# Gathering 20 of 731 row sets with TensorE: one-hot matrices times a table split into three bf16 parts

## The chip, the cores and the metric

The kernel runs on one core of a Trainium2 chip. Its time is the device time of one execution in microseconds (us), the median of several. Of the core's engines PE is TensorE, DVE VectorE, ACT ScalarE, POOL GpSimd and SP SyncE; SP computes nothing here and only issues transfers.

## What is computed

A graph of 6250 nodes and 100000 edges sorted by `dst`; D is 256. For each edge a vector from the source's and the destination's rows, then the maximum over the edges of each node, then a residual and a layer norm.

```python
x_src = x[src]
x_dst = x[dst]
theta_x = (x_dst - x_src) @ theta_w.T + theta_b
phi_x = x_src @ phi_w.T + phi_b
e = relu(theta_x + phi_x)
out = segment_max(e, dst, num_segments=x.shape[0])
out = where(isfinite(out), out, 0.0)
return layernorm(x + out)
```

Since `relu` is monotone and the part of `dst` is the same for all edges of a node, the kernel takes the maximum over `B[src]` alone, with B = x (phi - theta), and adds A = x theta + the two biases afterwards.

## The kernel before

The edges are cut into 128 runs of 782 edges, one run to a partition. Step k handles edge k of every run: it needs 128 rows of B (128x256 f32, 128 KB), which an indirect DMA of POOL gathers, and DVE folds them into a running maximum that restarts where `dst` changes (`reset`). The steps go in 261 groups of three.

Before the loop PE makes B in 49 tiles of 128 nodes (L411), ACT copies them out of PSUM (L357), SP writes them to `b_table` in HBM. Meanwhile POOL gathers 51 row sets of x itself into `early` (L303); in groups 0 to 102 PE transposes and multiplies them (L437, L427) and ACT copies them (L368, L366), so that the first step of the groups 6, 8, ... 106 needs no gather from the table. That leaves 731 gathers (L315) into `rows`, which has 18 places: POOL waits with a gather until the step that used its place is folded (`s_fold`).

In a group g of the loop, in the order of each queue: DVE folds three steps (L582), two into PSUM (`acc`) and the third into `hist`; every step waits for the one before through `s_fold`. ACT copies the two from `acc` to `hist` (L379). SP writes the group's three maxima to `runmax` in HBM (L274). The first step of group g waits for the gather and for ACT's copy of group g - 2 (`s_copied`), and a place of `hist` is free again when the write of group g - 6 has landed. Every fourth group up to 196 has a mark as well: two small DVE operations (L596, L601), five PE matmuls with the bf16 halves `hi` and `lo` of `dst` (L447 to L449), one ACT pass over 782 columns (L384). In groups 204 to 252 PE makes one tile of A each (L462) from `xt_sb` tiles that SP loads, and DVE adds the biases into `a_sb` (L631). After the last group the maxima that cross a run are mended, and in a tail of 14 pieces the maximum of each node is gathered from `runmax`, added, normalised and written; none of that is touched.

All queues are written out by hand and run in program order. PE, for one, does in group g: product and transposes of a conversion, the mark, the tile of A.

## Time and profile before

| | us |
|---|---|
| median of 3 runs (lowest, highest) | 1245.99 (1243.34, 1250.09) |
| the profiled execution | 1242.66 |
| its span, first to last instruction | 1240.8 |
| first and last row gather start | 103.8, 1143.6 |

The profile's page gives each engine's busy time, its share in 40 slices, the DMA queues, the chain that ended last and the groups of instructions. A row of the timeline is: start, duration, engine, line, operation, output and inputs, shape, count, and in brackets how long the engine was idle before and what ended that. "remote" and "issue" there mean that the profile shows no releaser.

### The profile page before, as it was taken

How to read it: one execution, taken by the hardware profiler on the slowest of the kernel's cores; microseconds unless marked ns; L12 is line 12 of the kernel's file. 1: busy time of each engine (PE TensorE's matmuls, PEld its weight loads, DVE VectorE, ACT ScalarE, POOL GpSimd, SP SyncE). 2: the span in 40 equal slices, each digit the busy share in tenths (PEclk: the TensorE clock that was granted, in tenths of full speed). 3: DMA queues.
4: the chain of work that ended last, by engine and by line, in shares of the span. 5: the costliest groups of instructions: out<-in, count | busy, mean ns of one | idle time of the engine just before them, and what ended most of it. 6: DMA issues, size and time to landing. Idle time of an engine off the chain costs nothing.

```text
span 1240.8 us, 5980 instructions
## 1 busy us (share of the span) xinstructions
PE 313.0 (25%) x953; PEld 194.2 (16%) x953; DVE 518.0 (42%) x1191; ACT 274.6 (22%) x568; POOL 807.9 (65%) x840
## 2 busy tenths in 40 slices
PE   6363322444342343110000000100014342430000
PEld 5142111222121232000000000000012131210000
DVE  4002332545343454543333433543325253537698
ACT  2022132233232232321111211321101010100144
POOL 6724756766666766677765676677746667667574
PEclk9667565666566655555555555555557565656555
DMA  8567545666465665676655665776547476747264
GB/s 262 164 196 225 178 156 169 229 204 210 159 204 181 215 213 194 231 241 201 199 191 166 209 192 191 256 228 206 192 139 261 145 236 225 240 136 229 100 195 157
DMA packets 111584, 245.76 MB, mean 198 GB/s; under 512 B 19141, under 2 KB 51226, under 8 KB 111546
## 3 DMA queue, kind: packets, MB, share of 16 engines
q0 software_dynamic: 39984, 109.21, 30.8%
q1 hardware_dynamic: 71130, 135.51, 29.9%
q10 hardware_dynamic: 432, 0.66, 0.2%
q14 instruction: 30, 0.25, 0.1%
q8 instruction: 8, 0.13, 0.0%
HBM read 129.89 MB, written 115.45 MB: 198 GB/s over the span
## 4 chain that ended last, share of the span: by engine, by line
DVE 29%; another core or an unknown queue 27%; issue 19%; POOL 10%; PE 6%; ACT 5%; DMA 4%; DVEq 1%; SPq 0%; ACTq 0%; POOLq 0%
DVE acc L582 16%; POOL rows L315 9%; DVE hist L582 6%; ACT hist L379 3%; DMA rows<-b_table,idx 2%; DVE stats L692 1%; PE acc L411 1%; DVE a_sb L681 1%; DVE hist L689 1%; DVE reached L596 1%; DVE a_sb L676 1%; PE ps_b L427 1%; PE ps_a L411 1%; DVEq L580 1%
## 5 line engine op out<-in xcount | busy, mean ns | idle before, releaser
L315 POOL DMA_INDIRECT rows<-b_table,idx x731 | 701.3, 959 | 372.2 <-issue 208.4
L379 ACT COPY hist<-acc 128x512 f32<-128x512 f32 x253 | 147.3, 587 | 471.0 <-DVE hist L582 241.3
L582 DVE SCALAR_TENSOR_TENSOR acc<-acc,reset,rows 128x256 f32<-128x256 f32 x253 | 124.7, 493 | 116.2 <-DVE acc L582 41.9
L582 DVE SCALAR_TENSOR_TENSOR acc<-hist,reset,rows 128x256 f32<-128x256 f32 x201 | 98.7, 491 | 151.5 <-issue 52.6
L582 DVE SCALAR_TENSOR_TENSOR hist<-acc,reset,rows 128x256 f32<-128x256 f32 x253 | 122.3, 483 | 80.8 <-DVE acc L582 41.0
L427 PE MATMUL ps_b<-diff_sb,conv_t 128*128 128x256 f32 x204 | 93.7, 607 | 223.5 <-issue 119.0
L447 PE MATMUL ps_d<-hi,row_of 128*128 128x512 bf16 x98 | 48.7, 497 | 381.3 <-remote 181.1
L462 PE MATMUL ps_a<-theta_sb,xt_sb 128*128 128x256 f32 x196 | 77.6, 545 | 130.6 <-issue 77.8
L427 PEld LDWEIGHTS ps_b<-diff_sb,conv_t 128*128 128x128 f32 x204 | 54.6, 295 | 243.0 <-issue 144.6
L582 DVE SCALAR_TENSOR_TENSOR acc<-hist,reset,early 128x256 f32<-128x256 f32 x51 | 25.2, 495 | 137.5 <-ACT hist L379 93.2
L384 ACT ACTIVATE signs<-ps_d,node_up 128x782 bf16<-128x782 f32 x49 | 44.7, 912 | 151.6 <-issue 74.6
L447 PEld LDWEIGHTS ps_d<-hi,row_of 128*128 128x128 bf16 x98 | 12.2, 124 | 409.7 <-remote 183.9
L462 PEld LDWEIGHTS ps_a<-theta_sb,xt_sb 128*128 128x128 f32 x196 | 47.2, 266 | 160.7 <-issue 154.5
L340 POOL DMA_INDIRECT rows<-runmax,end_row x49 | 53.1, 1083 | 16.3 <-issue 14.6
L303 POOL DMA_INDIRECT early<-in_x,idx x51 | 50.3, 985 | 18.9 <-issue 15.2
L631 DVE TENSOR_TENSOR a_sb<-ps_a,bias 128x256 f32<-128x256 f32 x49 | 20.4, 417 | 91.6 <-remote 77.2
L448 PE MATMUL ps_d<-lo,row_of 128*128 128x512 bf16 x98 | 49.3, 506 | 0.0
L366 ACT COPY early<-ps_b 128x256 f32<-128x256 f32 x50 | 18.7, 374 | 118.1 <-remote 93.2
L368 ACT COPY conv_t<-ps_t 128x256 f32<-128x256 f32 x51 | 19.2, 377 | 58.9 <-remote 37.8
L396 ACT ACTIVATE hist<-hist,shift,rstd 128x256 f32<-128x256 f32 x49 | 25.7, 590 | 29.2 <-DVE shift L661 18.7
L556 DVE TENSOR_SCALAR carry_on<-ps_b 128x128 f32<-128x128 f32 x1 | 0.3, 291 | 74.5 <-PE ps_b L417 74.5
L437 PE MATMUL ps_t<-ident,early 128*128 128x128 f32 x102 | 28.0, 371 | 0.7 <-DVE carry_on L557 0.7
(120 smaller groups left out, 342.9 us busy)
## 6 DMA issues: line engine op xcount, KB each, us to landing
runmax<-hist SPq DMA_DIRECT2D x260, 384.0 KB
rows<-b_table,idx POOLq DMA_INDIRECT x731
b_table<-rows SPq DMA_DIRECT2D x7, 896.0 KB
xt_sb<-in_xt SPq DMA_DIRECT2D x49, 128.0 KB
early<-in_x SPq DMA_DIRECT2D x12, 512.0 KB
out<-hist SPq DMA_DIRECT2D x11, 512.0 KB, 2.9
xt_sb<-in_xt SPq DMA_DIRECT2D x7, 512.0 KB
xt_sb<-in_xt SPq DMA_DIRECT2D x7, 384.0 KB
```

The costliest lines, as they stand in the source:

```text
L303: pool.indirect_dma_start(out=early[:, e, :], out_offset=None, in_=x, in_offset=bass.IndirectOffsetOnAxis(ap=idx[:, k:k + 1], axis=0)).the ...
L315: pool.indirect_dma_start(out=rows[:, PLACE[k], :], out_offset=None, in_=b_table, in_offset=bass.IndirectOffsetOnAxis(ap=idx[:, k:k + 1], ...
L340: pool.indirect_dma_start(out=rows[:, slot + i, :], out_offset=None, in_=runmax, in_offset=bass.IndirectOffsetOnAxis(ap=end_row[:, t + i:t ...
L379: nc.scalar.copy(hist[:, slot:slot + n - 1, :], acc[:, at:at + n - 1, :]).then_inc(s_copied, 1)
L384: nc.scalar.activation(signs[:], dst_rows[:, 0:STEPS], ACT.Sign, bias=node_up[:, t:t + 1], scale=-1.0, accum_out=in_row[:, t:t + 1]).then_ ...
L396: nc.scalar.activation(hist[:, i, :], hist[:, i, :], ACT.Identity, scale=rstd[:, i:i + 1], bias=shift[:, i:i + 1]).then_inc(s_norm, 1)
L427: mm = pe.matmul(ps_b[:, 0, :], conv_t[:, k, :], diff_sb[:, k, :], start=(k == 0), stop=(k == KC - 1))
L437: mm = pe.transpose(ps_t[:, 0, k * P:(k + 1) * P], early[:, e, k * P:(k + 1) * P], ident[:])
L447: pe.matmul(dst_rows[:, at:at + n], row_of[:], hi[:, at:at + n], start=True, stop=False)
L448: pe.matmul(dst_rows[:, at:at + n], row_of[:], lo[:, at:at + n], start=False, stop=True)
L462: mm = pe.matmul(ps_a[t % 2][:, 0, :], xt_sb[:, t % (2 * CHUNK), k, :], theta_sb[:, k, :], start=(k == 0), stop=(k == KC - 1))
L582: nc.vector.scalar_tensor_tensor(new, former, reset[:, k:k + 1], row_at(k), ALU.min, ALU.max).then_inc(s_fold, 1)
```

## The change

The rows of B for 20 steps, the first of 20 groups, are not gathered but computed by PE. A product takes four such steps at once, 512 edges: for each of the 49 table tiles a one-hot matrix `hot` (128 nodes x 512 edges, bf16) says which node of the tile is the source of which edge, and PE adds up, over all tiles, table tile times `hot` in PSUM. To keep f32 values the table stands in SBUF as three bf16 parts, whose sum it is, so there are 2 halves of D x 3 parts = 6 matmuls a tile. The result is transposed back and stands in `far`, from where DVE's step reads it.

Five such batches run over the groups 27 to 216, 38 groups each; tiles begin at the fifth group. Their rows are used in groups 71, 79, 87, 95; 109, 117, 125, 133; 147, 155, 163, 171; 185, 193, 201, 209; 223, 228, 233, 238. POOL makes 711 gathers.

What else there is: SP reloads the table in 25 pairs of tiles in groups 0 to 23 and loads the sources of each batch, broadcast to all partitions; ACT and DVE split the pairs into the three parts in groups 0 to 26; DVE makes the one-hots behind the steps of a group; ACT makes the sources int16, and copies products and transposes out. `hot` has four places. The tiles of A move to groups 220 to 244, two a group, since `xt_sb` and `a_sb` share their room with the parts; their x tiles are loaded at group 218, 14 at once. PE's queue has the tiles between the mark and the tile of A.

```diff
+SPLITS = 3
+AT_ONCE = 4
+HOT = 4
+PRODUCT_SPANS = ((27, 65, 8), (65, 103, 8), (103, 141, 8), (141, 179, 8), (179, 217, 5))
...
+    PAIRS = (NT + 1) // 2
+    PRODUCTS = len(PRODUCT_SPANS)
+    HOT_AT = {g: [] for g in range(NG)}
+    PRODUCT_OF = {}
+    BATCH_GROUPS = []
+    for b, (begin, stop, apart) in enumerate(PRODUCT_SPANS):
+        for t in range(NT):
+            HOT_AT[begin + 4 + t * (stop - begin - 4) // NT].append((b, t))
+        first = stop + 6 if stop % 2 else stop + 7
+        BATCH_GROUPS.append([first + apart * j for j in range(AT_ONCE)])
+        for j, g in enumerate(BATCH_GROUPS[b]):
+            assert START[g] not in EARLY_OF and g < NG and (b + 1 == PRODUCTS or g < PRODUCT_SPANS[b + 1][1] + 2)
+            PRODUCT_OF[START[g]] = (b, j)
+    SPLIT_BY = PAIRS + 2
+    EVACUATE_AT = {stop: b for b, (_, stop, _) in enumerate(PRODUCT_SPANS)}
+    TURN_AT = {stop + 1: b for b, (_, stop, _) in enumerate(PRODUCT_SPANS)}
+    FAR_AT = {stop + 2: b for b, (_, stop, _) in enumerate(PRODUCT_SPANS)}
+    SOURCES_AT = {begin - 6: b for b, (begin, _, _) in enumerate(PRODUCT_SPANS)}
+    SHORT_AT = {begin: b for b, (begin, _, _) in enumerate(PRODUCT_SPANS)}
...
-    A_AT = {204 + t: t for t in range(NT)}
+    A_FROM = PRODUCT_SPANS[-1][1] + 3
+    A_AT = {A_FROM + i: [t for t in (2 * i, 2 * i + 1) if t < NT] for i in range((NT + 1) // 2)}
...
-    GATHERED = [k for k in range(STEPS) if k not in EARLY_OF]
+    GATHERED = [k for k in range(STEPS) if k not in EARLY_OF and k not in PRODUCT_OF]
...
-        xt_sb = sb("xt_sb", [P, 2 * CHUNK, KC, P])
+        shared = sb("shared", [P, NT * D * SPLITS // 2])
+        xt_sb = shared[:, 0:2 * CHUNK * D].rearrange("p (j k n) -> p j k n", k=KC, n=P)
+        split = shared[:].bitcast(BF16).rearrange("p (s t d) -> p s t d", s=SPLITS, d=D)
+        a_sb = shared[:, 0:NT * D].rearrange("p (t d) -> p t d", d=D)
+        xt_late = shared[:, NT * D:(NT + 2 * CHUNK) * D].rearrange("p (j k n) -> p j k n", k=KC, n=P)
+        assert (NT + 2 * CHUNK) * D <= NT * D * SPLITS // 2
+        work = sb("work", [P, 8 * D])
+        b_pair = work[:, 0:4 * D].rearrange("p (i j d) -> p i j d", i=2, d=D)
+        rest = work[:, 4 * D:8 * D].rearrange("p (i j d) -> p i j d", i=2, d=D)
+        turned = work[:, 0:KC * AT_ONCE * P].rearrange("p (k e) -> p k e", k=KC)
+        hot = work[:, 4 * D:4 * D + HOT * AT_ONCE * P // 2].bitcast(BF16).rearrange("p (i e) -> p i e", i=HOT)
+        assert KC * AT_ONCE * P <= 4 * D and HOT * AT_ONCE * P // 2 <= 4 * D
+        far = sb("far", [P, AT_ONCE, D])
+        sources = sb("sources", [P, AT_ONCE, P], I32)
...
+            pairs = b_table.rearrange("(t p) d -> p t d", p=P)
+            by_step = src_t.rearrange("(a k) e -> a k e", a=1)
+
+            def load_pair(i):
+                if i >= 2:
+                    sp.wait_ge(s_rest, i - 1)
+                n = min(2, NT - 2 * i)
+                sp.dma_start(b_pair[:, i % 2, 0:n], pairs[:, 2 * i:2 * i + n]).then_inc(s_pair[i % 2], 16)
+
+            sp.wait_ge(s_bout[0], 16 * (CHUNKS + 1) // 2)
+            sp.wait_ge(s_bout[1], 16 * (CHUNKS // 2))
+            for i in range(2):
+                load_pair(i)
             for g in range(NG):
+                if 1 <= g < PAIRS - 1:
+                    load_pair(g + 1)
+                if g in SOURCES_AT:
+                    b = SOURCES_AT[g]
+                    if b:
+                        sp.wait_ge(s_short, b)
+                    k0, apart = START[BATCH_GROUPS[b][0]], START[BATCH_GROUPS[b][1]] - START[BATCH_GROUPS[b][0]]
+                    sp.dma_start(sources[:], by_step[:, k0:k0 + (AT_ONCE - 1) * apart + 1:apart, :].broadcast_to(
+                        [P, AT_ONCE, P])).then_inc(s_sources, 16)
+                if g == A_FROM - 2:
+                    sp.wait_ge(s_hotused, PRODUCTS * NT)
+                    for t in range(2 * CHUNK):
+                        load_tile(t)
                 n, slot = STOP[g] - START[g], g % HELD * GROUP
                 if g < LATE:
...
+                if 2 <= g < PAIRS + 2:
+                    i = g - 2
+                    n = min(2, NT - 2 * i)
+                    act.wait_ge(s_rest, i + 1)
+                    nc.scalar.copy(split[:, 1, 2 * i:2 * i + n, :], rest[:, i % 2, 0:n]).then_inc(s_split2, 1)
+                if g < PAIRS:
+                    n = min(2, NT - 2 * g)
+                    act.wait_ge(s_pair[g % 2], 16 * (g // 2 + 1))
+                    nc.scalar.copy(split[:, 0, 2 * g:2 * g + n, :], b_pair[:, g % 2, 0:n]).then_inc(s_split1, 1)
...
+                if g in SHORT_AT:
+                    b = SHORT_AT[g]
+                    act.wait_ge(s_sources, 16 * (b + 1))
+                    if b >= 2:
+                        act.wait_ge(s_hot, NT * (b - 1))
+                    nc.scalar.copy(short_sources[:, b % 2, :],
+                                   sources[:].rearrange("p k e -> p (k e)")).then_inc(s_short, 1)
+                if g in EVACUATE_AT:
+                    b = EVACUATE_AT[g]
+                    act.wait_ge(s_hotused, NT * (b + 1))
+                    if b:
+                        act.wait_ge(s_turned, b)
+                    for k in range(KC):
+                        nc.scalar.copy(turned[:, k, :],
+                                       ps_a[k][:].rearrange("p j d -> p (j d)")).then_inc(s_prodev, 1)
+                if g in FAR_AT:
+                    b = FAR_AT[g]
+                    act.wait_ge(s_turned, b + 1)
+                    if b:
+                        act.wait_ge(s_fold, START[BATCH_GROUPS[b - 1][-1]] + 1)
+                    for k in range(2):
+                        nc.scalar.copy(far[:, 2 * k:2 * k + 2, :], ps_a[k][:]).then_inc(s_far, 1)
 
...
+                for b, t in HOT_AT[g]:
+                    i = b * NT + t
+                    if i == 0:
+                        pe.wait_ge(s_split1, PAIRS)
+                        pe.wait_ge(s_split2, PAIRS)
+                        pe.wait_ge(s_split3, PAIRS)
+                    if t == 0 and b:
+                        pe.wait_ge(s_far, 2 * b)
+                    pe.wait_ge(s_hot, i + 1)
+                    for k in range(KC):
+                        for part in range(SPLITS):
+                            mm = pe.matmul(ps_a[k][:].rearrange("p j d -> p (j d)"),
+                                           split[:, part, t, k * P:(k + 1) * P], hot[:, i % HOT, :],
+                                           start=(t == 0 and part == 0), stop=(t == NT - 1 and part == SPLITS - 1))
+                    mm.then_inc(s_hotused, 1)
+                if g in TURN_AT:
+                    b = TURN_AT[g]
+                    pe.wait_ge(s_prodev, KC * (b + 1))
+                    for j in range(AT_ONCE):
+                        for k in range(KC):
+                            mm = pe.transpose(ps_a[j // 2][:, j % 2, k * P:(k + 1) * P],
+                                              turned[:, k, j * P:(j + 1) * P], ident[:])
+                    mm.then_inc(s_turned, 1)
...
-                if g in A_AT:
...
+                for t in A_AT.get(g, []):
                     pe.wait_ge(s_at[t % (2 * CHUNK)], 16 * (t // (2 * CHUNK) + 1))
+                    if t == 0:
+                        pe.wait_ge(s_far, 2 * PRODUCTS)
...
+                if START[g] in PRODUCT_OF:
+                    dve.wait_ge(s_far, 2 * PRODUCT_OF[START[g]][0] + 2)
...
+                if 2 <= g < PAIRS + 2:
+                    i = g - 2
+                    n = min(2, NT - 2 * i)
+                    dve.wait_ge(s_split2, i + 1)
+                    nc.vector.tensor_tensor(split[:, 2, 2 * i:2 * i + n, :], rest[:, i % 2, 0:n],
+                                            split[:, 1, 2 * i:2 * i + n, :], ALU.subtract).then_inc(s_split3, 1)
+                if 1 <= g < PAIRS + 1:
+                    i = g - 1
+                    n = min(2, NT - 2 * i)
+                    dve.wait_ge(s_split1, i + 1)
+                    if i >= 2:
+                        dve.wait_ge(s_split3, i - 1)
+                    nc.vector.tensor_tensor(rest[:, i % 2, 0:n], b_pair[:, i % 2, 0:n],
+                                            split[:, 0, 2 * i:2 * i + n, :], ALU.subtract).then_inc(s_rest, 1)
+                for b, t in HOT_AT[g]:
+                    i = b * NT + t
+                    dve.wait_ge(s_short, b + 1)
+                    if i >= HOT:
+                        dve.wait_ge(s_hotused, i - HOT + 1)
+                    elif i == 0:
+                        dve.wait_ge(s_split3, PAIRS)
+                    nc.vector.tensor_scalar(hot[:, i % HOT, :], short_sources[:, b % 2, :], node[:, t:t + 1], None,
+                                            ALU.is_equal).then_inc(s_hot, 1)
...
+                for t in A_AT.get(g, []):
```

## Rows read from the trace of the kernel before

**Rows 1.** The page, part 1: busy time, share of the span, instructions.

```profile
PE 313.0 (25%) x953; PEld 194.2 (16%) x953; DVE 518.0 (42%) x1191; ACT 274.6 (22%) x568; POOL 807.9 (65%) x840
```

**Rows 2.** The gather's line by itself: ns min/median/max, first and last start.

```profile
L315 POOL DMA_INDIRECT rows<-b_table,idx x731: 941/947/1208, 103.8 to 1143.6; - x183
```

**Rows 3.** Who waited for whom, POOL: us in total, times, longest.

```profile
POOL rows L315 <- issue: 208.4, 661, 3.3
POOL rows L315 <- DVE hist L582: 91.9, 44, 9.8
POOL rows L315 <- DVE acc L582: 27.6, 23, 6.3
```

**Rows 4.** Busy time by stage: length, engines (instructions), TensorE clock, DMA share, GB/s.

```profile
103.50:222.50 119.00, 34.26 (x100) 21.33 (x101) 42.46 (x93) 27.50 (x62) 79.01 (x83) 0.55 0.58 187
222.50:514.00 291.50, 108.43 (x329) 66.88 (x327) 127.00 (x281) 87.56 (x197) 189.79 (x200) 0.60 0.60 198
514.00:924.00 410.00, 38.64 (x127) 16.78 (x127) 154.68 (x348) 79.58 (x143) 283.80 (x295) 0.50 0.63 204
924.00:1154.00 230.00, 74.79 (x190) 44.94 (x190) 107.84 (x247) 29.31 (x50) 149.74 (x156) 0.60 0.63 207
```

**Rows 5.** Timeline while B is made: POOL's last x gathers, ACT's copies.

```profile
70.08 0.94 POOL L303 DMA_INDIRECT early<-in_x,idx  x1 [0.30 <-issue]
...
74.19 0.37 ACT L357 COPY rows<-ps_d 128x256 f32<-128x256 f32 x1 [10.83 <-remote]
...
77.78 0.65 ACT L357 COPY rows<-acc 128x256 f32<-128x256 f32 x2 [3.21 <-PE ps_d L411]
```

**Rows 6.** Timeline of a conversion: PE's product, ACT's copy, POOL's gathers around it.

```profile
148.46 2.07 PE L427 MATMUL ps_b<-diff_sb,conv_t 128*128 128x256 f32 x4 [7.80 <-issue]
...
165.38 0.95 POOL L315 DMA_INDIRECT rows<-b_table,idx  x1 [0.30 <-issue]
...
170.44 0.37 ACT L366 COPY early<-ps_b 128x256 f32<-128x256 f32 x1 [7.62 <-remote]
...
176.13 0.95 POOL L315 DMA_INDIRECT rows<-b_table,idx  x1 [9.80 <-DVE hist L582]
```

**Rows 7.** Timeline at the tiles of A: PE's product, DVE's addition.

```profile
963.80 2.05 PE L462 MATMUL ps_a<-theta_sb,xt_sb 128*128 128x256 f32 x4 [7.06 <-issue]
...
973.72 0.42 DVE L631 TENSOR_TENSOR a_sb<-ps_a,bias 128x256 f32<-128x256 f32 x1 [8.55 <-remote]
```

**Rows 8.** Timeline, DVE's steps, two neighbours in each of two places.

```profile
604.73 0.49 DVE L582 SCALAR_TENSOR_TENSOR acc<-hist,reset,rows 128x256 f32<-128x256 f32 x1 [0.26 <-DVE hist L582]
...
606.73 0.49 DVE L582 SCALAR_TENSOR_TENSOR acc<-acc,reset,rows 128x256 f32<-128x256 f32 x1 [1.50 <-DVE acc L582]
...
820.15 0.49 DVE L582 SCALAR_TENSOR_TENSOR acc<-hist,reset,rows 128x256 f32<-128x256 f32 x1 [2.16 <-DMA rows<-b_table,idx]
820.68 0.49 DVE L582 SCALAR_TENSOR_TENSOR acc<-acc,reset,rows 128x256 f32<-128x256 f32 x1
```

**Rows 9.** Timeline of a mark's matmuls; busy time of a stretch with PE busy.

```profile
183.94 0.39 PE L447 MATMUL ps_d<-hi,row_of 128*128 128x512 bf16 x1 [2.56 <-issue]
...
184.17 0.38 PE L448 MATMUL ps_d<-lo,row_of 128*128 128x512 bf16 x1
...
938.00:950.00 12.00, 7.19 (x26) 4.27 (x24) 10.32 (x25) 3.51 (x7) 9.26 (x10) 0.96 0.96 328
```

**Rows 10.** Groups nearest to the added work; DMA issues: KB each, us to landing.

```profile
L596 DVE TENSOR_SCALAR reached<-cols_b,first_node 128x128 bf16<-128x128 bf16 x49 | 13.0, 266 | 0.0
L491 DVE TENSOR_TENSOR diff_sb<-diff_sb,theta_sb 128x512 f32<-128x512 f32 x1 | 0.7, 693 | 9.7 <-DMA diff_sb<-in_phi_t 9.7
L379 ACT COPY hist<-acc 128x512 f32<-128x512 f32 x253 | 147.3, 587 | 471.0 <-DVE hist L582 241.3 <-issue 128.3 <-DVE acc L582 82.6
...
theta_sb<-in_theta_t SPq DMA_DIRECT2D x1, 256.0 KB, 5.9
...
out<-hist SPq DMA_DIRECT2D x1, 256.0 KB, 2.1
```

More of the change, by code:

```diff
@@ L11 @@
 I32 = mybir.dt.int32
+I16 = mybir.dt.int16
 AX_X = mybir.AxisListType.X
@@ L20, with build @@
 EARLY = 51
-def build(nc, x, xt, src, dst, theta_t, phi_t, theta_b, phi_b, out):
+SPLITS = 3
+AT_ONCE = 4
+HOT = 4
+PRODUCT_SPANS = ((27, 65, 8), (65, 103, 8), (103, 141, 8), (141, 179, 8), (179, 217, 5))
+def build(nc, x, xt, src, src_t, dst, theta_t, phi_t, theta_b, phi_b, out):
     N, D = x.shape
@@ L102, in build @@
         x_sb = early[:, 0:NT, :]
-        a_sb = sb("a_sb", [P, NT, D])
         rows = sb("rows", [P, SLOTS, D])
@@ L116, in build @@
         last_node = sb("last_node", [P, NT])
+        node = sb("node", [P, NT])
         node_up = sb("node_up", [P, NT])
@@ L197, in build @@
         s_inrow = sem("edges_compared_in_row")
+        s_pair = [sem(f"table_pair_loaded{i}") for i in range(2)]
+        s_split1 = sem("first_parts_made")
+        s_rest = sem("rests_made")
+        s_split2 = sem("second_parts_made")
+        s_split3 = sem("third_parts_made")
+        s_sources = sem("sources_loaded")
+        s_short = sem("sources_shortened")
+        s_hot = sem("one_hots_made")
+        s_hotused = sem("one_hots_used")
+        s_prodev = sem("products_evacuated")
+        s_turned = sem("products_turned")
+        s_far = sem("turned_products_evacuated")
         s_edges = sem("edges_up_to_nodes")
@@ L228, in _ @@
             by_chunk = xt.rearrange("(c j) p k n -> c p j (k n)", j=CHUNK)
-            xt_flat = xt_sb[:].rearrange("p j k n -> p j (k n)")
+            xt_flat = xt_sb.rearrange("p j k n -> p j (k n)")
+            late_flat = xt_late.rearrange("p j k n -> p j (k n)")
             table = b_table.rearrange("(c j p) d -> c p j d", j=CHUNK, p=P)
@@ L260, in load_tile @@
                     sp.wait_ge(s_amm, t - 2 * CHUNK + 1)
-                sp.dma_start(xt_flat[:, t % (2 * CHUNK)],
+                sp.dma_start(late_flat[:, t % (2 * CHUNK)],
                              xt[t].rearrange("p k n -> p (k n)")).then_inc(s_at[t % (2 * CHUNK)], 16)
-            sp.wait_ge(s_bmm, NT)
-            for t in range(2 * CHUNK):
-                load_tile(t)
-            for g in range(NG):
+            pairs = b_table.rearrange("(t p) d -> p t d", p=P)
[9 more added lines that the diff above has]
+                load_pair(i)
+            for g in range(NG):
+                if 1 <= g < PAIRS - 1:
[11 more added lines that the diff above has]
+                        load_tile(t)
                 n, slot = STOP[g] - START[g], g % HELD * GROUP
@@ L280, in _ @@
                     sp.dma_start(x_sb[:, i * X_TILES:(i + 1) * X_TILES, :], by_load[i]).then_inc(s_x, 16)
-                if g in A_AT and A_AT[g] + 2 * CHUNK - 2 < NT and A_AT[g] >= 2:
-                    load_tile(A_AT[g] + 2 * CHUNK - 2)
+                if g - 1 in A_AT:
+                    for t in A_AT[g - 1]:
+                        if t + 2 * CHUNK < NT:
+                            load_tile(t + 2 * CHUNK)
             out_tiles = out[0:(NT - 1) * P].rearrange("(t p) d -> p t d", p=P)
@@ L461, in _ @@
                     for k in range(KC):
-                        mm = pe.matmul(ps_a[t % 2][:, 0, :], xt_sb[:, t % (2 * CHUNK), k, :], theta_sb[:, k, :],
+                        mm = pe.matmul(ps_a[t % 2][:, 0, :], xt_late[:, t % (2 * CHUNK), k, :], theta_sb[:, k, :],
                                        start=(k == 0), stop=(k == KC - 1))
@@ L504, in _ @@
             then(nc.vector.tensor_scalar(small[:, 11:12], part[:], 0.5, None, ALU.add))
+            nc.vector.tensor_scalar(node[:], cols[:, 0:NT], float(P), part[:, 0:1], ALU.mult, ALU.add)
             nc.vector.tensor_scalar(node_up[:], cols[:, 0:NT], float(P), small[:, 11:12], ALU.mult, ALU.add)
@@ L560, in row_at @@
             def row_at(k):
+                if k in PRODUCT_OF:
+                    return far[:, PRODUCT_OF[k][1], :]
                 return rows[:, PLACE[k], :] if k in PLACE else early[:, EARLY_OF[k], :]
@@ L573, in _ @@
                         dve.wait_ge(s_got_end, 16)
-                    elif k in PLACE and (s == 0 or START[g] in EARLY_OF and s == 1):
+                    elif k in PLACE and (s == 0 or START[g] not in PLACE and s == 1):
                         dve.wait_ge(s_got[g % LANDED], ARRIVED[g])
@@ L700, in _ @@
             scales(len(TAIL) - 1)
-_INS = ["x", "xt", "src", "dst", "theta_t", "phi_t", "theta_b", "phi_b"]
+_INS = ["x", "xt", "src", "src_t", "dst", "theta_t", "phi_t", "theta_b", "phi_b"]
 def kernel(x, src, dst, L0_gnn_theta_w, L0_gnn_theta_b, L0_gnn_phi_w, L0_gnn_phi_b):
@@ L726 @@
     arrays = {
-        "x": x, "xt": xt, "src": by_p.reshape(P, steps), "dst": windows,
+        "x": x, "xt": xt, "src": by_p.reshape(P, steps),
+        "src_t": by_p.reshape(P, steps).T, "dst": windows,
         "theta_t": np.asarray(L0_gnn_theta_w).T, "phi_t": np.asarray(L0_gnn_phi_w).T,
```

5 lines of the change are left out of this document (2 added, 3 removed).

## The prediction

> **What bounds the kernel now.** The page's first part comes first: no engine is busy more than 65% of the span, and that one is POOL [rows 1]. So the view to read next is POOL's own line. One row gather costs it 0.947 us in the median and 731 of them are 701 us [rows 2]; between two of them lie 0.30 us in which nothing is waited for (208.4 us in 661 places, [rows 3]). A gather that waits for nothing therefore takes 1.25 us of POOL, and 731 take 914 us. The gathers run from 103.8 to 1144.6 us, so some 127 us are something else: POOL waiting for a free place among the 18 in `rows`, which is DVE's fold (91.9 and 27.6 us, [rows 3]; 11.4 more stand under "remote" in the same list). By stage, counts times 1.25 us against the length of the stage: 250 of 291.5 us while x rows are converted, 369 of 410 us in the middle, 194 of 230 us at the A tiles, of which 9 lie behind the last gather [rows 4]. POOL's issue is the floor, and about one eighth of the loop is the chain behind it falling more than 18 steps back.
>
> Why does it fall back? Nothing there is short of engine time: a step is 0.49 us, three in a group are 1.8 us where nothing is waited for, against 3.75 us of POOL for three gathers. What is late are signals. While the table is made, POOL issues x gathers without a break until 71 us; ACT, which copies PE's products out, stands for 10.83 us before its copy at 74.19, and from 77.78 us on, when POOL has stopped, two copies follow at once [rows 5]; a product is 2.07 us of PE [rows 6]. The same at the conversions: PE's product that starts at 148.46 us is over near 150.5; ACT's copy of it starts at 170.44, 20 us later, 4 us after POOL ran out of places (its last gather starts at 165.38, the next at 176.13) [rows 6]. At the A tiles the product that starts at 963.80 us (2.05 us) is taken by DVE at 973.72, 7.9 us after its end [rows 7]. All engines stand still in such a pause. I read them together: with POOL issuing without a break for some 10 us or more and PE having results that others wait for, a result of PE takes 8 us or more to get through, one in 8 to 11 us, and all at once when POOL stops. In the middle, where PE has one short job in four groups, a milder form sits on DVE: a step starts 1.99 us after the one before it where it is 0.53 us elsewhere [rows 8]. The trace doesn't say by what mechanism.
>
> **The change part by part.** All of it is set against the profiled execution, 1242.66 us with a span of 1240.8, 3.3 us under the median of 1245.99, and the difference is then added to the median.
>
> Removed: 20 gathers of 1.25 us, 25.0 us of POOL's time. Of the 20, 4 (groups 71 to 95) lie in the conversion stage, 12 (109 to 209) in or just behind the middle, 4 (223 to 238) in the last stage. They are worth 25 us only if POOL's waits stay as they are; where POOL is 18 steps ahead anyway, a gather less is only a longer wait.
>
> Added on PE: 5 batches of 49 tiles, six matmuls of 512 columns each, 1470 in all. The 512-column bf16 matmul of `hi` and `lo` is followed by the next after 0.23 us [rows 9]. I take that as the higher clock level, 2.4 GHz; at the lower, 1.2 GHz, an estimate is twice that. That makes a tile 1.4 or 2.8 us, and all of them 338 or 676 us. PE is busy 108 and 39 us in the two stages that hold the work now and some 20 behind them [rows 4], and groups 27 to 217 are some 760 us, so the fast end fits and the slow one is over it by a tenth. I take the fast end: where PE is kept busy the granted share is 0.96 [rows 9]. There are 49 tiles in 34 groups, 1.44 in a group: 2.0 us of PE in each, and 4.0 us at the slow end. Together with its own work (108 us in 80 groups, 1.4 us) a group in a burst takes PE 3.4 us or more, where DVE now runs through bursts of groups at 1.8 us.
>
> Added on DVE: 245 comparisons of 512 int16 columns. The nearest row is 128 bf16 columns in 0.27 us [rows 10]; between that and four times that, 1.1 us; I take 0.4, since at 0.27 most is fixed, so 0.6 us in a group and 98 us in all; DVE is busy 127 of 291.5 and 155 of 410 us [rows 4]. Bounded by 3.75 us in a group it hides under POOL. But DVE then waits for PE: a comparison needs the place of the fourth tile before it (`s_hotused`), and behind it in DVE's queue stand the steps of the next group, for which POOL's places and ACT's copies wait. Until now no step waited for PE directly in groups 27 to 203.
>
> This is the term that decides. PE's signals that somebody needs rise from 1.25 in a group (two per conversion in every other group, one per mark in four) to 2.5 in the conversion stage, and from 0.25 to 1.5 in the middle. POOL's stop is what frees them. Now there are some 27 gathers between two long stops (200 gathers and 40 us of waits of up to 6.3 us in the conversion stage, 7 or 8 stops of 5.5 us). After the change fewer groups pass between two stops, since a burst is 3.4 us in a group instead of 1.8 and the late phase lets half as many groups through: I take 20 gathers. In the conversion stage, 196/20 = 9.8 stops of 5.5 us are 54 us against 41.5: +12. Between groups 107 and 217, 318/20 = 15.9 stops are 87 us against 41 in the middle and some 11 behind it: +35. Bounds of this term: -60 us if a busier PE ends the lateness altogether (about what is waited there now), +150 us if every stop comes after 12 gathers.
>
> Moved: A tiles, from one a group in groups 204 to 252 to two a group in 220 to 244. The same 49 products and additions, but two results of PE for each group; groups 245 on get free. +5 us, from -5 to +25.
>
> Added at the start, groups 0 to 26: 25 reloads of two table tiles (256 KB each), two ACT copies of 128x512 (0.59 us each, [rows 10]) and two DVE subtractions (0.69 us each, [rows 10]) a group. Their engine time, 1.2 and 1.4 us, hides under 3.1 us of POOL. The ring does not: subtraction in group g, load of pair g+1 behind it on SP, ACT's copy in group g+1 ahead of the copy of that group's maxima. A 256 KB transfer landed in 2.1 to 5.9 us [rows 10]; 4 + 0.6 + 0.7 + DVE's 3.2 us for two groups is 8.5 us against 7.5 us of POOL in two. ACT holds its queue meanwhile (`conv_t`, `early`, the copy that frees `acc`), and SP's `runmax` writes stand behind `s_rest`. +8 us, from 0 to +40. The loads and the five broadcasts of 256 KB add 7.7 MB and 20 gathers take off 2.6 MB, 5.1 MB on balance, beside DMA engines that are busy 0.6 of the time [rows 4]: nothing.
>
> Ends of batches: two copies, 8 transposes, two copies, five times. PE's transposes and ACT's copies have two groups of time; +3 us, from 0 to +25. XT loads, 14 at once at group 218, replace loads far ahead: nothing while they land before group 220, up to +5. I hold that in the range.
>
> Sum: -25 + 12 + 35 + 5 + 8 + 3 = +38 us, 1279 us of span, 1284 us against the median.
>
> A rule of the Trainium skill speaks against this change in another way. In this trace the gathers that run beside a step with both tensors in SBUF are the ones that take up to 1.21 us instead of 0.95 [rows 2], and those beside the 128-column comparison are not longer. The Trainium skill (SBUF - State Buffer, section SBUF: two separate sides) says that VectorE in a two-port mode locks GpSimd out of the port pair that it needs to write descriptors, so a gather waits until VectorE's operation is over. By its rule an int16 comparison out of SBUF into bf16 would hold POOL each time; the row of the short comparison doesn't show it.
>
> **The rivals.** (a) POOL's issue decides and the chain keeps up: the waits stay where they are, the new work hides. For it: PE and DVE have the time, and there are stretches in which DVE waits for the gather itself ([rows 8], second pair: 2.16 us before the step). Against it: the 127 us of waits have a cause that isn't engine time. -25 + 5 for the start = 1226 us. With PE's lateness gone as well, down to 1180. Chance 0.35.
> (b) The gathers were hidden at both ends: in the stretches where POOL is a full ring ahead the 25 us turn into waits, the rest pays for the start. 1240 to 1252 us. Chance 0.12.
> (c) The forecast, slower by one mechanism: PE's late signals are now in DVE's queue in groups 27 to 217. It decides from the point where a cycle between two stops of POOL holds fewer than some 23 gathers (25 us are 4.5 stops of 5.5 us; now they are 731/27 = 27, and 711 gathers in 31.5 stops are 22.6 each). 1255 to 1330 us. Chance 0.33.
> (d) The same mechanism in full: during a late phase each of the 1.5 to 2.5 signals takes 8 to 11 us and the four places of `hot` are used up in 3 groups, so that DVE stands until POOL has stopped; 12 gathers a stop, 1330 to 1450 us. Chance 0.15.
> (e) The port rule: each comparison holds a gather for its own 0.4 us, 245 x 0.4 = 98 us at most, half of them met: +49 - 20 = 1275 us. Chance 0.05, as the 128-column rows don't show it.
> That the change doesn't do what it says is no case: the steps' rows come from `far` by a fixed table.
>
> **How the numbers follow.** The likeliest sign is slower, (c), (d) and (e), 0.53; faster 0.35; within 0.5% (6.2 us, about what a measurement of this kernel can tell) 0.12. The predicted time is 1284 us. The likeliest case's own range is 1255 to 1330. For 8 in 10 the range must take in (a) without its lower tail and a part of (d): 1215 to 1370 us.
>
> **What would show it.** Right: the count of POOL's gathers 711, their mean unchanged near 0.95 us (longer means (e)); POOL's waits for DVE over 160 us instead of 131; new waits of the comparison or the next step for PE of several us; ACT's copies at group ends waiting for PE. PE busy some 650 to 990 us in all (313 now and 338 to 676 more) at a granted share over 0.8. Wrong: POOL's waits at or under 130 us and gathers following each other at 1.25 us through groups 107 to 217. Then the lateness either didn't follow PE's work or went with it, and the time is near 1226. If groups 0 to 26 take more than 150 us (119 now), the ring of the reloads is mis-sized.

## The result, and the profile after

The changed kernel took 1282.1 us in the median (1279.3 to 1285.2) beside 1244.7 us (1240.6 to 1250.1) for the kernel before: ratio 1.0292, 95% interval 1.0244 to 1.0339. The forecast was 1284 us, slower. The profiled execution's span is 1282.5 us, with a granted TensorE clock of 0.715 against 0.573.

The page's first part and its line of the gather (busy, mean ns | idle before it, releasers):

```profile
PE 657.1 (51%) x2463; PEld 337.5 (26%) x2463; DVE 615.8 (48%) x1487; ACT 306.1 (24%) x643; POOL 797.3 (62%) x820
...
L395 POOL DMA_INDIRECT rows<-b_table,idx x711 | 691.3, 972 | 420.9 <-issue 204.8
```

No engine is near its limit, as in [rows 1]; POOL's share even fell. What grew stands in the waits (us in total, times, longest), first two lines of the kernel before, then the change's. Each is idle time of the engine in front of the instruction named:

```profile
ACT early L366 <- remote: 93.2, 14, 9.1
...
ACT signs L384 <- remote: 57.6, 9, 12.4
```

```profile
POOL rows L395 <- issue: 204.8, 645, 5.6
DVE work L756 <- remote: 186.7, 40, 8.8
ACT signs L473 <- remote: 159.1, 12, 20.6
ACT early L455 <- remote: 146.5, 16, 15.1
...
POOL rows L395 <- DVE acc L723: 110.0, 39, 7.3
...
POOL rows L395 <- DVE hist L723: 72.8, 24, 7.3
```

POOL's waits for DVE's folds are 183 us (110.0 and 72.8) where they were 120 [rows 3]. DVE's comparison (L756) and ACT's two readers of PE's results (L473 at the marks, L455 at the conversions) wait 492 us together under "remote"; the same two readers had 151 us before, and the comparison did not exist. Counted as in the prediction, as start to start of POOL's gathers over 1.25 us each, POOL lost 127 us before and 191 after: +64. Stops of over 1 us went from 24 (112 us in all) to 39 (169 us); that is 30 gathers a stop before and 18 after, and a mean stop of 4.7 and 4.3 us.

This count over the 1.25 us each is called POOL's excess below.

Busy time by stage, from DVE's first step of group 27 to that of group 103, and from there to group 204; the columns are those of [rows 4]:

```profile
231.80:522.40 290.60, 215.82 (x901) 109.94 (x900) 147.83 (x365) 83.93 (x194) 176.39 (x183) 0.85 0.56 184
522.40:965.30 442.90, 242.22 (x925) 98.68 (x924) 195.77 (x491) 87.27 (x166) 283.10 (x293) 0.74 0.59 194
```

The first stage of [rows 4] ends later, at group 107, so the lines can't be set beside each other as they are. Between the same two steps, groups 27 to 103 took 283.6 us before, in which 192 gathers started, and take 290.6 with 183; groups 103 to 204 took 417.9 us with 300 gathers and take 442.9 with 292. One stop in the middle, by timeline (DVE, PE, ACT, POOL; start, length, [idle before <- releaser]):

```profile
564.28 0.35 DVE L756 TENSOR_SCALAR work<-short_sources,node 128x512 bf16<-128x512 int16 x1 [5.17 <-remote]
...
575.48 0.35 DVE L756 TENSOR_SCALAR work<-short_sources,node 128x512 bf16<-128x512 int16 x1 [8.78 <-remote]
576.23 0.35 DVE L756 TENSOR_SCALAR work<-short_sources,node 128x512 bf16<-128x512 int16 x1 [0.40 <-remote]
...
566.59 2.72 PE L574 MATMUL ps_a<-work,shared 128*128 128x512 bf16 x6
575.89 7.10 PE L574 MATMUL ps_a<-work,shared 128*128 128x512 bf16 x24 [6.58 <-DVE work L756]
...
576.30 0.91 ACT L473 ACTIVATE signs<-ps_d,node_up 128x782 bf16<-128x782 f32 x1 [16.58 <-remote]
...
571.72 0.94 POOL L395 DMA_INDIRECT rows<-b_table,idx  x1 [0.30 <-issue]
577.78 0.95 POOL L395 DMA_INDIRECT rows<-b_table,idx  x1 [5.12 <-DVE acc L723]
```

PE finishes a tile's six matmuls at 569.3. DVE's next comparison starts at 575.48, 2.8 us after POOL's last gather is over; then all goes at once. Counted through the 1470 matmuls and 245 comparisons of the trace, it needs the place of the fourth tile before it, and that tile's last matmul was over at 554.4: the signal came 21 us late. The comparisons before it, at 557.24 and 564.28, got theirs 5.4 and 11.2 us late. PE's matmuls themselves aren't slow here: the mark's five and the tile's six follow each other in the usual way while POOL issues. It is the picture of [rows 5 to 7], now also in the middle.

### The profile page after: what moved, and what is told of

The parts are those of the page before. It is cut to its first block, busy times and chain, and to the rows that moved or that the text cites. A ratio compares the mean times of both kernels' runs of the same rounds, so it can differ in the third digit from the quotient of the medians.

```text
span 1282.5 us, 9685 instructions
## 1 busy us (share of the span) xinstructions
PE 657.1 (51%) x2463; PEld 337.5 (26%) x2463; DVE 615.8 (48%) x1487; ACT 306.1 (24%) x643; POOL 797.3 (62%) x820
## 4 chain that ended last, share of the span: by engine, by line
another core or an unknown queue 35%; DVE 20%; issue 17%; PE 16%; ACT 5%; POOL 4%; DMA 3%; DVEq 1%; SPq 0%; ACTq 0%; POOLq 0%
DVE acc L723 8%; PE ps_a L574 7%; POOL rows L395 4%; PE ps_a L598 3%; DVE hist L723 3%; ACT hist L468 2%; DVE work L756 2%; DVE stats L855 1%; DVE shared L844 1%; DVE hist L852 1%; DVE shared L839 1%; PE acc L523 1%; PE ps_a L523 1%; DMA work<-b_table 1%
## 5 line engine op out<-in xcount | busy, mean ns | idle before, releaser
L395 POOL DMA_INDIRECT rows<-b_table,idx x711 | 691.3, 972 | 420.9 <-issue 204.8
L574 PE MATMUL ps_a<-work,shared 128*128 128x512 bf16 x1470 | 396.0, 428 | 154.7 <-DVE work L756 85.8
L574 PEld LDWEIGHTS ps_a<-work,shared 128*128 128x128 bf16 x1470 | 149.3, 107 | 375.0 <-issue 149.7
L756 DVE TENSOR_SCALAR work<-short_sources,node 128x512 bf16<-128x512 int16 x245 | 86.3, 369 | 224.6 <-remote 186.7
L539 PE MATMUL ps_b<-diff_sb,conv_t 128*128 128x256 f32 x204 | 76.5, 512 | 93.7 <-ACT conv_t L457 63.8
L723 DVE SCALAR_TENSOR_TENSOR acc<-hist,reset,rows 128x256 f32<-128x256 f32 x181 | 88.1, 487 | 75.4 <-ACT hist L468 37.9
L473 ACT ACTIVATE signs<-ps_d,node_up 128x782 bf16<-128x782 f32 x49 | 45.0, 918 | 222.0 <-remote 159.1
L598 PE MATMUL ps_a<-theta_sb,shared 128*128 128x256 f32 x196 | 65.8, 494 | 50.0 <-issue 41.0
L598 PEld LDWEIGHTS ps_a<-theta_sb,shared 128*128 128x128 f32 x196 | 46.0, 249 | 69.7 <-issue 62.2
L455 ACT COPY early<-ps_b 128x256 f32<-128x256 f32 x50 | 18.7, 374 | 178.1 <-remote 146.5
L794 DVE TENSOR_TENSOR shared<-ps_a,bias 128x256 f32<-128x256 f32 x49 | 20.2, 421 | 61.2 <-remote 41.1
L560 PE MATMUL ps_d<-lo,row_of 128*128 128x512 bf16 x98 | 38.2, 405 | 0.0
```

The source lines that it names most:

```text
L395: pool.indirect_dma_start(out=rows[:, PLACE[k], :], out_offset=None, in_=b_table, in_offset=bass.IndirectOffsetOnAxis(ap=idx[:, k:k + 1], ...
L473: nc.scalar.activation(signs[:], dst_rows[:, 0:STEPS], ACT.Sign, bias=node_up[:, t:t + 1], scale=-1.0, accum_out=in_row[:, t:t + 1]).then_ ...
L539: mm = pe.matmul(ps_b[:, 0, :], conv_t[:, k, :], diff_sb[:, k, :], start=(k == 0), stop=(k == KC - 1))
L560: pe.matmul(dst_rows[:, at:at + n], row_of[:], lo[:, at:at + n], start=False, stop=True)
L574: mm = pe.matmul(ps_a[k][:].rearrange("p j d -> p (j d)"), split[:, part, t, k * P:(k + 1) * P], hot[:, i % HOT, :], start=(t == 0 and par ...
L598: mm = pe.matmul(ps_a[t % 2][:, 0, :], xt_late[:, t % (2 * CHUNK), k, :], theta_sb[:, k, :], start=(k == 0), stop=(k == KC - 1))
```

## The experiments

Ratios are to the kernel before on the same chip in the same session. Two theories are set against each other: **theory 1**, the prediction's, that a late answer of PE now stands in DVE's queue; **theory 2**, formed from the trace of `free_wait` below and so put to the test only from `one_mm` on, that the late stretch lets PE's instructions through in slots of some 0.70 us, so that their number counts. The expectations of `one_mm` and `double` name a third, that PE's column time or its clock is what costs.

**The parts without the products.** `a_moved`: the change's A tiles (two in a group from 220 on) and memory layout, no table parts, no products, all 731 gathers.

> The kernel before, with only what the change moves: the tiles of A two a group in groups 220 to 244, and the new layout of SBUF. 731 gathers, no reload of the table, no products. Theory (the sum of the prediction): +5 us on the kernel before, 1250, from 1240 to 1262. If the moved tiles are the loss: 1270 or more.

Measured 1251.5 us, ratio 1.0031 [0.9988, 1.0074]: no difference that can be told.

`start`: that, with the reload and splitting of the table in groups 0 to 26.

> As a_moved, with the reload of the table and its splitting into three parts in groups 0 to 26, and no products, 731 gathers. It prices the start alone. Theory: +8 us on a_moved, all of it before group 27. Rival (the ring of load, copy and subtraction sets the pace of the first groups): +25 to +40 us.

Measured 1254.7, ratio 1.0077 [1.0030, 1.0125], 3 us over `a_moved` (6 by the ratios). From DVE's first step to that of group 27 it takes 121.6 us instead of 114.7 in `a_moved`.

`fewer`: `a_moved` without the 20 gathers (the 20 steps fold a constant row, so these edges are missing).

```
         for j, g in enumerate(BATCH_GROUPS[b]):
...
-            pass
+            PRODUCT_OF[START[g]] = (b, j)
```

> As a_moved, but the 20 gathers are left out and nothing is in their place: the 20 steps fold a constant row of very negative numbers, so those edges are missing from the output. It prices the 20 gathers alone. Theory: POOL's issue is the floor, its waits for DVE stay about as they are, so 15 to 25 us under a_moved, 1225 to 1235. Rival (the gathers were hidden where POOL is a full ring ahead): 0 to 10 us under a_moved.

Measured 1223.2, ratio 0.9780 [0.9699, 0.9860], 28 us under `a_moved` (31 by the ratios, and uncertain by some 11), where 15 to 25 were expected. The 20 gathers are worth their full 25 us; POOL's excess stays about the same, 129 us for 133. So what the products themselves cost is 1282 less (1223 and 3 to 6 for the start), some 55 us.

**DVE never waits for PE.** `free_wait`: the comparison writes into spare places and PE multiplies a constant zero one-hot, with all matmuls, comparisons and signals in place (the rows of the 20 steps are zero).

```
-                    if i >= HOT:
-                        dve.wait_ge(s_hotused, i - HOT + 1)
...
+                    if i >= HOT - 1:
+                        dve.wait_ge(s_hot, i - HOT + 2)
```

> The changed kernel with all its work, all 1470 matmuls, 245 comparisons and 245 signals of PE, but DVE never waits for PE's use of a one-hot: PE multiplies a one-hot matrix of zeros and the comparisons go to places that nobody reads, so the rows of the 20 steps are zeros. Theory (the loss is DVE waiting for PE's late signals): most of the 47 us of new waits goes, 1232 to 1255. Rivals (time of PE or DVE, or the comparisons holding POOL through the port): it stays at 1275 to 1285, since all of that work is still there.

Measured 1308.0, ratio 1.0474 [1.0392, 1.0555]: slower than the change. Theory 1 missed by over 50 us, and so did, by over 20, the rivals of the expectation. Its waits, and then, by timeline, PE beside ACT's mark and POOL in one late stretch:

```profile
DVE acc L723 <- ACT hist L468: 308.4, 25, 27.3
ACT signs L473 <- remote: 231.3, 15, 25.5
```

```profile
562.96 0.16 PE L561 MATMUL ps_d<-p_col,row_of 128*128 128x1 bf16 x1 [1.14 <-issue]
565.75 0.58 PE L574 MATMUL ps_a<-work,shared 128*128 128x512 bf16 x1 [2.62 <-issue]
567.85 0.58 PE L574 MATMUL ps_a<-work,shared 128*128 128x512 bf16 x1 [1.52 <-issue]
569.95 0.59 PE L574 MATMUL ps_a<-work,shared 128*128 128x512 bf16 x1 [1.52 <-issue]
572.08 0.58 PE L574 MATMUL ps_a<-work,shared 128*128 128x512 bf16 x1 [1.54 <-issue]
574.88 0.58 PE L574 MATMUL ps_a<-work,shared 128*128 128x512 bf16 x1 [2.22 <-issue]
...
583.27 8.11 PE L574 MATMUL ps_a<-work,shared 128*128 128x512 bf16 x22 [0.82 <-issue]
...
584.25 0.91 ACT L473 ACTIVATE signs<-ps_d,node_up 128x782 bf16<-128x782 f32 x1 [25.41 <-remote]
...
578.88 0.95 POOL L395 DMA_INDIRECT rows<-b_table,idx  x1 [0.30 <-issue]
587.05 0.95 POOL L395 DMA_INDIRECT rows<-b_table,idx  x1 [7.23 <-DVE acc L723]
```

While POOL issues, PE's matmuls start 2.1, 2.1, 2.1 and 2.8 us apart, three and four times 0.70 us, and wait for nothing the profile knows ("issue"). Over the whole trace, 189 spacings of the tiles' matmuls lie between 0.6 and 3.8 us, and 135 of them within 0.04 us of 0.7, 1.4, 2.1, 2.8 or 3.5. In the change's own trace it is 6 of 64: there PE is seldom caught with matmuls to start, and what is late is the signal of matmuls that are over. From 583.27, after POOL's last gather ended at 579.8, 22 of them take 8 us. The mark's matmuls were over at 563.1; ACT reads the result at 584.25. With DVE's wait gone, the wait turned up at ACT, which stands ahead of DVE's steps through `acc`.

**How many instructions PE has in a tile.** `one_mm`: one matmul a tile instead of six (the 20 rows lack most of their sum), all 245 comparisons, waits and signals kept.

```
                     for k in range(KC):
-                        for part in range(SPLITS):
+                        if t % KC != k and t < NT - 2:
+                            continue
...
```

> The change with one matmul of 512 columns a tile where it has six (two in the last two tiles of a batch); every one-hot, every wait and every signal stay, 245 of each. The rows of the 20 steps lack most of their sum. Theory 1 (what costs is the lateness of a tile's answer, one in 8 to 11 us whatever is in it): the stages of groups 27 to 217 stay within 10 us of the change's, 1265 to 1285 us. Theory 2 (what costs is the number of PE's instructions that stand ahead of a needed answer, each taking a slot of about 0.70 us while POOL issues without a break): a tile takes 3 or 4 slots where it took 14 to 16, the marks' answers come on time, 1228 to 1248 us. Theory 3 (PE's column time, or the clock): likewise about 1240, but then the kernel with doubled instructions at the same column time costs nothing.

Measured 1245.9, ratio 1.0007 [0.9971, 1.0043]. It is within theory 2's range and 19 us under theory 1's.

`double`: a one-column matmul, with its own weight load, ahead of each of the 1470 but ten (it adds one column a second time).

```
+                            if t or part:
+                                pe.matmul(ps_a[k][:, 0, 0:1], split[:, part, t, k * P:(k + 1) * P],
+                                          hot[:, i % HOT, 0:1], start=False, stop=False)
```

> The change with a second matmul of one column, and so a second weight load, ahead of 243 in 245 first parts and all others: twice the instructions of PE a tile at 1/512 more column time (the first of a tile group's four edges counts a column twice, its value is wrong). Theory 1 (answers late whatever is in them) and theory 3 (PE's column time): within 10 us of the change, 1275 to 1292 us. Theory 2 (instructions in slots of 0.70 us): a tile takes some 28 slots, about 20 us, in a late stretch, so POOL's stops grow and number more: 1320 to 1400 us.

Measured 1308.7, ratio 1.0529 [1.0468, 1.0590]; 51 stops of POOL of 3.9 us. Against a kernel without products (`fewer` and what the start adds by the ratios, 0.983), 255 matmuls cost 1.8%, 1470 cost 4.6%, 2930 cost 7.0%: 22, 58 and 87 us of 1247. Signals and comparisons are the same 245 in all three, so theory 1's fixed lateness of an answer is out. From 255 to 1470 the column time grows with the count; from 1470 to 2930 it hardly does, only matmul instructions and weight loads, and `double` is 17 us over what theories 1 and 3 allowed. So PE's instructions cost. But the cost isn't in proportion: theory 2 hit `one_mm`, and `double` fell 11 us short of its low end. In quick stretches a pair of `double` takes 0.24 us where one matmul takes 0.22, and PE is busy 56%; I can't divide the 30 us between the slots and this.

`hot8`: eight places for one-hots instead of four; they take the room of `turned` as well, so a batch's first comparison waits for the transposes of the batch before.

```
-HOT = 4
+HOT = 8
...
```

> The change with eight places for one-hots in place of four (a batch's first comparison then waits for the transposes of the batch before). VectorE can be eight tiles ahead of PE before it waits, so more of PE's work can pile up ahead of a mark. Theory 1 (VectorE's wait for a late answer in front of a fold): that wait falls away for most tiles, 1250 to 1272 us. Theory 2 (PE's backlog ahead of the marks and conversions): no gain, the wait turns up at ScalarE's marks as in the kernel where VectorE never waited, 1278 to 1310 us.

Measured 1298.6, ratio 1.0393 [1.0325, 1.0461], 1% over the change, which is only just clear of the noise. More room is no gain and rather a loss:

```profile
ACT signs L473 <- remote: 241.7, 16, 25.4
```

ACT's marks wait that long for PE instead of 159.1 us, and PE's matmuls are back in the slots (142 of 203 spacings). I read it that the ring of four was a brake that kept PE's backlog ahead of the marks short.

**POOL paced by PE while B is made.** `paced` is the kernel before with one more wait.

```
             for k, e in EARLY_OF.items():
+                if e >= 4:
+                    pool.wait_ge(s_bmm, min(e - 3, NT))
```

> The kernel before with one more wait: POOL issues the gather of early step e (from 4 on) only when B tile e-3 is in PSUM, so that it stops by itself whenever PE falls behind while B is made. Nothing else changes. Theory 2: PE gets through without slots whenever POOL waits, so B is complete earlier than at 99 us (some 85 to 90), and the kernel takes 1230 to 1245 us beside 1249. Theory 1 (the lateness is a fixed one of each answer, and is not PE's throughput): each wait costs POOL one late answer of about 11 us and the kernel takes 1250 to 1290.

Measured 1222.9 (1219.2 to 1225.6), ratio 0.9808 [0.9761, 0.9854]: it beats both kernels. The first row gather starts at 86.6 us instead of 103.8. The stretch 20 to 60 us by the columns of [rows 4], of the kernel before, then of `paced`, and some of the latter's x gathers by timeline:

```profile
20.00:60.00 40.00, 20.81 (x79) 15.73 (x77) 4.84 (x17) 4.92 (x14) 30.31 (x32) 0.72 0.66 212
```

```profile
20.00:60.00 40.00, 31.61 (x128) 24.31 (x126) 4.39 (x17) 9.68 (x26) 27.65 (x29) 0.91 0.84 271
```

```profile
44.39 0.95 POOL L305 DMA_INDIRECT early<-in_x,idx  x1 [0.49 <-PE ps_d L413]
45.82 0.95 POOL L305 DMA_INDIRECT early<-in_x,idx  x1 [0.48 <-PE acc L413]
47.93 0.95 POOL L305 DMA_INDIRECT early<-in_x,idx  x1 [1.17 <-PE ps_t L413]
```

Theory 1's 1250 to 1290 is out, theory 2's 1230 to 1245 lies 7 us too high. Three gathers fewer and pauses of 0.2 to 1 us beyond the usual 0.30 let PE do 128 matmuls instead of 79.

**A shorter look-ahead.** Would such pauses help in the main loop too?

```
-                if last >= SLOTS:
-                    pool.wait_ge(s_fold, GATHERED[last - SLOTS] + 1)
+                if last >= 8:
+                    pool.wait_ge(s_fold, GATHERED[last - 8] + 1)
```

> The kernel before with the look-ahead of the gathers cut from 18 to 8: POOL issues a group only when all but the last 8 gathered rows have been folded (the ring of 18 stays). Theory 2 (results come late only while POOL issues without a break; pauses of 0.2 to 1.3 us kept them on time while B was made in the paced kernel): POOL pauses shortly and often, fewer late stretches arise, 1190 to 1240 us. Rival (a late stretch arises all the same after some 12 us, and POOL now stops 10 gathers sooner in each, 12.5 us earlier, with the same 4 to 5 us of stop): the stops double in number, 1290 to 1350.

> The paced kernel (early gathers wait for B tile e-3) with the look-ahead cut to 8 as well. If the two act in different stages their effects add: the time is that of the kernel with look-ahead 8 less 17 to 24 us (what pacing gave while B is made). If late stretches are carried over from one stage into the next, more than that.

> The change, with both: early gathers that wait for B tile e-3, and a look-ahead of 8. The products need 6 x 0.43 = 2.6 us of PE in 3.1 us of tile spacing, so PE has little to spare. Theory 2: with results on time the change's cost falls from +37 to at most +10 us against the paced kernel of look-ahead 8, and may turn into a gain of up to 20. Rival (PE's own time is what the products cost): still +30 to +40 against it.

All three ran on a chip on which the kernel before takes 1081.5 us (1080.0 to 1082.8 in 11 runs) instead of 1246. Measured there: `ahead8` 1084.2, ratio 1.0030 [1.0016, 1.0044]; `paced8` 1087.2, 1.0055 [1.0038, 1.0072]; `after_paced8` 1090.9, 1.0093 [1.0077, 1.0110]. The waits of `ahead8`, and its busy time in 20 to 60 us:

```profile
POOL rows L315 <- issue: 202.0, 663, 0.3
POOL rows L315 <- DVE hist L582: 14.9, 48, 0.6
POOL rows L315 <- DVE acc L582: 7.8, 20, 1.6
...
DVE acc L582 <- DMA rows<-b_table,idx: 435.7, 215, 15.5
```

```profile
20.00:60.00 40.00, 37.78 (x172) 31.95 (x170) 5.19 (x18) 13.41 (x43) 30.25 (x33) 1.00 1.03 362
```

POOL issues as steadily as ever (33 gathers in these 40 us), and PE does 172 matmuls beside it at full clock. In the loop POOL's excess is 6 us in all, and DVE waits for the gathers, not POOL for DVE. No result is late: the list of waits has no "remote" at all. So none of the ranges for `ahead8` could be tried here, and `paced8`, expected 17 to 24 us under `ahead8`, is 3 us over it: where nothing is late, pacing gives nothing (the first row gather starts at 73.9 us instead of 69.8). Here the loop is POOL's issue, as rival (a) has it, and the span is 161 us shorter than before's 1240.8: 34 up to the first row gather (69.8 us instead of 103.8), 121 in POOL's excess, 6 elsewhere. The lateness belongs to the chip, or to the state it is in, and not to the program alone. The change gains nothing even here, with both edits in it: `after_paced8` is 1.0034 times `paced8`, +4 us. That is within the +10 of theory 2, though it was meant for a chip with late results; and the rival's +30 to +40, PE's own time as the price, is out. Its gathers give 25 us, but POOL's excess is 33.7 us against 7.7, 11 of the 26 more in groups 0 to 26; it holds the longer gathers too, 963 ns in the mean against 953. So 29 us of cost (the 25 gained, and 4) stand here with no late result, beside 62 on the other chips. The look-ahead of 8 may have a part in them; the change with 18 wasn't run on this chip.

The look-ahead was therefore tried once more, on another chip.

> The kernel with both, paced early gathers and look-ahead 8, a second time, because in the runs before it the kernel before took 1081 us instead of 1246 and no result came late, so that nothing was told of late stretches. If the kernel before takes some 1246 us here: theory 2 with short pauses that keep results on time gives 1130 to 1205 (paced with look-ahead 18 took 1223); the rival, that a late stretch arises all the same and POOL then stops 10 gathers sooner, gives 1250 to 1330. If the kernel before takes some 1081 us: 1.004 to 1.007 of it, as before, and the question stays open.

Here the kernel before took 1256.6 us. Measured: 1232.9 (1227.8 to 1239.7), ratio 0.9810 [0.9755, 0.9864], the ratio of `paced`. The look-ahead of 8 gives nothing and takes nothing. POOL now starts a group 3 to 5 rows ahead of DVE's steps nearly always, and stops sooner:

```profile
566.66 0.94 POOL L317 DMA_INDIRECT rows<-b_table,idx  x1 [2.86 <-remote]
...
571.62 0.94 POOL L317 DMA_INDIRECT rows<-b_table,idx  x1 [1.51 <-issue]
...
587.12 0.94 POOL L317 DMA_INDIRECT rows<-b_table,idx  x1 [3.62 <-issue]
```

39 stops of 3.1 us (120 us) stand where `paced` has 27 of 4.4 (118 us). Both sides of my expectation missed: short pauses didn't keep the loop free of late stretches, and stopping sooner didn't double the loss. How long POOL must stand still in the loop hangs on neither the length nor the number of the pauses that I tried.

## Why the prediction was right

The time and the sign were right, and POOL's more frequent stops were the reason, as forecast. What makes them more frequent was put in the wrong place. That the time came within 2 us is partly luck: the conversion stage and the middle were 8 and 4 us too low, and the start and the last stages too high. POOL's excess below is by the gathers' groups.

- **Removed gathers**: -25 forecast; -28 by `fewer` against `a_moved`. The guess that they aren't hidden held: POOL's excess doesn't change without them.
- **A tiles**: +5; `a_moved` shows +2.5 us, not told from nothing. In the change itself POOL's excess in groups 217 to 245 is 17.5 us instead of 15.0, and behind them 3 instead of 7.
- **Start**: +8; 3 to 6 by `start`, POOL's excess in groups 0 to 26 +6. The ends of the batches, +3, were not measured by themselves.
- **Conversion stage and groups 107 to 217**: +12 and +35. POOL's excess rose by 20 in groups 27 to 102 and by 39 in 103 to 216. The stop rate was as forecast in kind (18 gathers a stop for 20, from 30 for 27), with stops of 4.3 us and not 5.5; a burst runs at 1.8 to 2.4 us a group and not at 3.4. So the argument "a slower burst frees fewer groups" wasn't what made the stops more frequent.
- **PE's own time**: 344 us more, as the fast end had it (338). Of the signs named, POOL's waits for DVE (over 160 us: 183) came true, and the granted share over 0.8 did not: it is 0.715, and 0.85 and 0.74 in the two stages with the products.
- **The step that failed** is "PE's late signals are now in DVE's queue", with `s_hotused` as the deciding wait. The wait is there (186.7 us under "remote"), but the time doesn't hang on it: without it the kernel is 1.8% slower still, and with eight places 1%. What the products bring is PE instructions ahead of results that ACT and DVE needed already: the marks, the conversions. The prediction priced the right thing, a PE result that is late while POOL issues, by the number of signals (1.25 to 2.5 in a group); the runs with 1, 6 and 12 matmuls a tile, at the same signals, show that its instructions carry at least part of the price.
- **Rival (a)**, 1226 us, is what the kernel would do with the products free: `fewer` plus the start is 1226 to 1229. It is wrong by what the products cost. On the chip without lateness POOL's issue sets the pace, as it says, but the change doesn't get the 20 us there either (+4 us, with the look-ahead of 8).
- **Rival (e)**, the port rule: the gathers' median is 949 ns against 947 [rows 2] and their mean 972 against 959, 9 us over 711. Half of that lies in groups 0 to 26, where no comparison runs and DVE subtracts (952 to 1006 ns in the mean). An estimate by the Trainium skill (SBUF — State Buffer, section SBUF: two separate sides), whose lock would hold POOL through each of 245 comparisons of 0.35 us, is up to 86 us. The trace shows about a tenth of that, 9 us.
- **The premise**: the prediction read the lateness from one trace as what this kernel does. It is what this kernel does on three of the four chips that the experiments ran on, and in the measurements before them, with an eighth of the time in it (165 of 1246 us), and not on the fourth.

What stays open: by what mechanism PE's instructions and signals are held in late stretches, and whether the slots seen with a backlog and the late signals of the change are one thing; why one chip shows none; and why a short look-ahead changes nothing in the loop while pacing works where B is made. That the change, on a chip that is late, would gain from paced early gathers as the kernel before does wasn't tried.

## What to carry to other kernels

When no engine is full and results arrive late only while GpSimd issues indirect DMAs back to back, count the instructions queued on the engine whose results are late; moving work there, even off its critical path and far under its busy limit, can add to the waits behind it. A shorter ring can be better than a longer one: it bounds that queue, and a wait you remove can come back at the next reader of the same engine. Try letting the issuing engine pace itself by the consumer in stages where nobody needs its lead (one wait: 1.9% gained here, and nothing gained on the chip without lateness), and time a change on more than one chip before you call a limit a property of the program.

## What the hardware showed

- Late stretches: with POOL issuing an indirect DMA every 1.25 us, a result of PE was read up to 21 us after it was done (`free_wait` at 584.25, the change at 575.48). Where PE had a backlog its matmuls started 2.1 and 2.8 us apart, and 135 of 189 such spacings in `free_wait` were multiples of 0.70 us; in the change 6 of 64. It ended 3 to 4 us after POOL's last gather.
- The same kernel takes 1081 us on one chip and 1245 to 1257 on others. The gather's own time is 946 ns in the median on the one (`ahead8`) and 947 on the other (before), so POOL's issue doesn't tell them apart; PE's count in 20 to 60 us does (172 and 79, in stretches in which the two kernels do the same).
- An int16 comparison of 512 columns into bf16 took 0.35 us, under the 0.4 assumed, and 128x512 matmuls in bf16 followed each other at 0.22 us where the granted clock was 1.00 (2.4 GHz).
